# Moving twice as many of the sort's scatters behind the layers' gathers in a four-layer graph network kernel

## The reference

```python
# layer 0: mean of neighbours
mean = segment_sum(x[src], dst) / max(count, 1)
out  = l2_normalise(mean @ W_l + b_l + x @ W_r)
# layer 1: a weight matrix for each edge type
hw   = einsum('ni,rio->rno', x, weight)
out  = relu(segment_sum(hw[type, src] * edge_weight, dst) + bias)
# layer 2: five rounds of a gated cell on a state of 256
m    = h @ W[l];  agg = segment_sum(m[src], dst)
h    = GRU(agg, h)                        # then a two-layer MLP on [h, x]
# layer 3: an MLP on every edge, summed by source
h    = silu([x[src], x[dst], edge_attr] @ eW1 + eb1)
m    = silu(h @ eW2 + eb2)
agg  = segment_sum(m, src)                # then a node MLP on [x, agg]
```

## Time and profile before

| what | value |
|---|---|
| median of three runs | 9513.58 us (9509.02 to 9513.96) |
| the profiled execution's own time | 9513.96 us |
| its span from first to last instruction | 9511.7 us |
| mean granted TensorE clock | 0.819 |
| busy: PE, DVE, ACT, POOL | 64%, 60%, 27%, 72% |
| sort, until the first gather of layer 0 | 0 to 1165.0 us |
| first gathers of layer 1 and of layer 2 | 2210.6 us, 3208.8 us |
| first gather of the edge stage | 8435.2 us |

### The profile page before, as it was taken

One profiled execution on the slowest core, in us unless ns is written; L12 is line 12 of the kernel. 1 busy time (PEld: TensorE's weight loads), 2 busy tenths in 40 slices (PEclk: granted clock), 3 DMA queues, 4 the chain that ended last, 5 costly groups with the idle time before them and its releaser, 6 DMA issues. The chain is left out here.

```text
span 9511.7 us, 154496 instructions
## 1 busy us (share of the span) xinstructions
PE 6059.4 (64%) x34456; PEld 5100.5 (54%) x34457; DVE 5681.1 (60%) x13795; ACT 2535.7 (27%) x6529; POOL 6821.3 (72%) x7393
## 2 busy tenths in 40 slices
PE   0000055554444577777777777777776787779998
PEld 0000043333333466656666566656665666668887
DVE  9999644543444455545555555545554555556666
ACT  4212111112333111111111111111111333346665
POOL 1677377777777777777777777777777766677776
PEclk8555566665555699989999899989998999989999
DMA  2000022222222333333333333333333333322223
GB/s 67 6 7 7 29 78 80 78 78 77 60 60 59 84 111 111 111 98 111 111 111 104 105 111 111 111 98 111 112 111 97 109 100 100 96 54 63 64 64 54
DMA packets 377439, 786.63 MB, mean 83 GB/s; under 512 B 120397, under 2 KB 201394, under 8 KB 376731
## 3 DMA queue, kind: packets, MB, share of 16 engines
q0 software_dynamic: 289440, 677.19, 25.8%
q10 hardware_dynamic: 58500, 64.01, 2.2%
q1 hardware_dynamic: 29173, 42.12, 1.5%
HBM read 698.56 MB, written 84.29 MB: 82 GB/s over the span
## 5 line engine op out<-in xcount | busy, mean ns | idle before, releaser
L937 POOL DMA_INDIRECT rows<-state_table,rec x3910 | 3729.6, 954 | 1278.3 <-issue 1169.7
L1000 PE MATMUL l_prod<-rows,onehot 128*125 x11648 | 2979.0, 410 | 1739.2 <-SPq L949 698.5
L1025 DVE TENSOR_TENSOR agg<-agg,l_prod 125x256 f32 (+2 forms) x5824 | 2235.4, 384 | 2853.6 <-PE l_prod L1000 1889.4
L1000 PEld LDWEIGHTS l_prod<-rows,onehot 128*125 128x125 f32 x11648 | 2232.9, 226 | 2283.4 <-issue 2053.1
L1965 POOL DMA_INDIRECT l_gathered<-xcol_table,l_slots x832 | 785.6, 944 | 264.3 <-issue 250.5
L937 POOL DMA_INDIRECT rows<-rel_table,rec x782 | 738.7, 945 | 247.8 <-issue 237.7
L937 POOL DMA_INDIRECT rows<-in_x_dram,rec x782 | 738.8, 945 | 242.0 <-issue 234.0
L416 POOL DMA_INDIRECT slots_table<-rec_stage,row_stage x560 | 548.5, 980 | 172.4 <-issue 152.9
L1545 PE MATMUL l_rh<-state,w_hh_t 128*128 x4000 | 620.1, 292 | 1.8 <-ACT l_ng L1683 1.8
L1545 PEld LDWEIGHTS l_rh<-state,w_hh_t 128*128 128x128 f32 x4000 | 578.7, 210 | 16.2 <-ACT l_ng L1683 3.4
L1007 DVE TENSOR_TENSOR onehot<-l_rest,rec 128x500 f32<-128x500 f32 x835 | 560.7, 672 | 0.0
(11 more groups left out here) (359 smaller groups left out, 9741.0 us busy)
## 6 DMA issues: line engine op xcount, KB each, us to landing
rows<-state_table,rec POOLq DMA_INDIRECT x3910
rel_table<-l_relrow ACTq DMA_DIRECT2D x50, 500.0 KB
state_table<-l_row ACTq DMA_DIRECT2D x200, 125.0 KB
l_gathered<-xcol_table,l_slots POOLq DMA_INDIRECT x832
rows<-in_x_dram,rec POOLq DMA_INDIRECT x782
rows<-rel_table,rec POOLq DMA_INDIRECT x782
slots_table<-rec_stage,row_stage POOLq DMA_INDIRECT x560, 2.1
slots_table<-fill SPq DMA_DIRECT2D x8, 936.0 KB
```

What stands on the lines that cost most here:

```text
L937: pool.indirect_dma_start(out=K["rows"][:, r, 0:width], out_offset=None, in_=table, in_offset=bass.IndirectOffsetOnAxis(ap=K["rec"][:, c, ...
L1000: last = pe.matmul(p[0:LANES, 0:width], K["onehot"][:, h % ONEHOTS, k, :], rows[:, bass.ds(at[k], width)], start=True, stop=True)
L1025: dve.tensor_tensor(into, into, of, ALU.add).then_inc(S.added, 1)
```

## The change

`LATE` goes from 224 to 448 columns, so that 336 instead of 560 columns are scattered in the sort. Their shares: layer 0 from 44 to 66, layer 1 from 10 to 66, each of the first four rounds of layer 2 from 28 to 66, the last round from 58 to 52. `late_all`, the table `late` and `late_rec` take the new sizes.

```diff
-LATE = 224
-LATE_LAYER0, LATE_LAYER1, LATE_ROUND, LATE_LAST = 44, 10, 28, 58
-assert LATE_LAYER0 + LATE_LAYER1 + 4 * LATE_ROUND + LATE_LAST == LATE
+LATE = 448
+LATE_LAYER, LATE_ROUND, LATE_LAST = 66, 66, 52
+assert 2 * LATE_LAYER + 4 * LATE_ROUND + LATE_LAST == LATE
...
-            late.load(sp, LATE_LAYER0)
+            late.load(sp, LATE_LAYER)
...
-            late.scatter(pool, LATE_LAYER0, 1)
+            late.scatter(pool, LATE_LAYER, 1)
...
-            late.load(sp, LATE_LAYER1)
+            late.load(sp, LATE_LAYER)
...
-            late.scatter(pool, LATE_LAYER1, 2)
+            late.scatter(pool, LATE_LAYER, 2)
...
-                ("late_rec", [128, max(LATE_LAYER0, LATE_LAYER1, LATE_ROUND, LATE_LAST), REC_LATE]))
+                ("late_rec", [128, max(LATE_LAYER, LATE_ROUND), REC_LATE]))
```

## The result

| | median | runs | range |
|---|---|---|---|
| before | 9513.55 us | 4 | 9509.02 to 9513.96 |
| after | 9787.47 us | 4 | 9785.98 to 9798.5 |

The ratio is 1.0293, with a 95% interval from 1.0277 to 1.0308: 273.9 us or 2.9% slower. The forecast was 276.3 us.

The account below looks back on a forecast made before the run. GpSimd's stream of gathers was taken to bound layers 0 and 1 and four rounds, VectorE the sort. Terms 0 + 19.4 + 63.5 + 193.4 + 0 = 276.3 us gave 9790 us, range about 9768 to 9812.

Parts of the forecast that it names:

- What bounds it: Layers 0 and 1 and four of five rounds last as long as GpSimd's gather stream; additions there cost full length.
- Sort, 0: Sort: VectorE sets its end, so 224 fewer GpSimd scatters gain 0; gain bounded by 251 us.
- rival 3: Sort: VectorE was held up by GpSimd, so the sort would shrink by 251 us, to 9539; 2 in 100.
- rival 4: Sort: its end follows GpSimd's, so the barrier comes 324 us earlier, 9466 us, faster; 1 in 100.
- Late pieces on ScalarE, 0: Sort: ScalarE's twice as long late copies and the doubled record write fit in idle time and cover; cost 0.
- Layer 0 to 1 and layer 1 to 2, +19.4 and +63.5: Layer boundaries: added scatters first use up 8.4 and 7.5 us of shadow, then delay the next gather by these amounts.
- shadow left behind the scatters: Layer 0 to 1: time from the last scatter's end to the barrier, 8.4 us, counted as cover for added scatters.
- Rounds, +193.4: Between rounds: no shadow left, so 38 more scatters cost 48.3 us in full, four times.
- Last round to edge stage, 0: Last boundary: six fewer scatters end 7.6 us earlier, but the stores set the barrier, so 0.
- SP and its queue, 0: Rounds: record loads growing from 28 to 66 do not delay GpSimd; 0, bounds 0 and 20 us.
- Rival 1, TensorE's clock: Rounds: longer pauses lower TensorE's clock until it becomes the bound, 130 us more, 9920 us; 6 in 100.
- Rival 2, hidden rounds: Rounds: the drains hide the added scatters, so only layers 0 and 1 pay, 9597 us; 3 in 100.

Follow-up runs that it names:

- e3: Kernel before with 80 more late scatters: layer 0 to 66, layer 1 to 66, last round to 60, rounds kept at 28; 9633.52 us, ratio 1.0110.
- e4: Kernel before with 80 more late scatters, all behind the four rounds (28 to 48 each), layers unchanged; 9636.5 us, ratio 1.0112.
- e1: Kernel before with only a mask (& 255) on the two counts loaded for waits; 9531.95 us, ratio 1.0004 to before.
- e7: Changed kernel's sort side alone: 336 sort scatters, 448 columns loaded, but only 44, 10, 28 four times and 52 scattered late; 9509.71 us, ratio 0.9999 to before.
- e2: Changed kernel with a mask (& 255) added on the two counts loaded for waits; 9818.88 us, ratio 1.0305 to before.
- e5: Kernel before with 192 late scatters instead of 224 (layer 0 42, layer 1 5, rounds 23 each, last 53); 9481.15 us, ratio 0.9970.
- e6: Kernel before with 144 late scatters instead of 224 (layer 0 40, layer 1 2, rounds 14 each, last 46); 9479.51 us, ratio 0.9968.
- e8: Kernel before with GpSimd waiting for its late scatters to land at the ends of layers 0 and 1; 9525.16 us, one run.

## Why the prediction was right, and which step was not

- **What bounds it.** Right for the four rounds and layer 1, and nearly for layer 0, where the trace of before has 15 waits for ring space, 8.0 us in all. The last round, which the prediction did not count among them, waits 70 times for it, 99.7 us. What is put into GpSimd's stream behind the gathers costs its full length: e3 and e4 show 80 scatters at 104.4 and 107.4 us, that is 1.31 and 1.34 each by the medians and 1.27 to 1.30 by the gaps (e4's four rounds +101.8, e3's three boundaries +103.9 over e1).
- **Sort, 0.** Right. e7 isolates it at a ratio of 0.9999. The predicated copy takes 578 ns without scatters beside it, as it did with them. So rival 3 falls, and rival 4 with it: the barrier did not follow GpSimd. The rule of the Trainium skill (SBUF — State Buffer, "Who interferes with whom"), by which two-input VectorE instructions contend with GpSimd's reads, does not appear on VectorE's side in these traces: over a stretch in which GpSimd had been 251 us busy, VectorE's end moved by 1.9 us in the changed kernel (1163.08 to 1161.17) and 1.0 us in e7. Over all traces it lies at 1161.2 to 1162.5 us with 336 scatters in the sort (three) and at 1163.1 to 1163.4 with 560 (three), so a gain of 1 to 2 us is possible, against a bound of 251. Whether GpSimd's issuing of a scatter is a read in the sense of that rule, no run shows.
- **Late pieces on ScalarE, 0.** Right. SP's wait for the longer write is 12.1 us (reckoned 13) and stays inside the cover. The piece grew by 0.78 us (bound +0.97) and the next copy follows without an idle gap, where 0.82 us had been:

```profile
1039.93 1.75 ACT L455 COPY late_all<-attr 128x1792 f32<-128x1792 f32 x1
1041.73 0.60 ACT L488 COPY rec<-rec 112x448 f32<-112x448 f32 x1
```

- **Layer 0 to 1 and layer 1 to 2, +19.4 and +63.5.** The step that failed. I took "shadow left behind the scatters: 8.4 us" and 7.5 us from the distance between scatter and barrier, and gave it to the stores. It belonged to GpSimd's drain and moves with the last scatter. The full counts, 22 x 1.264 = 27.8 and 56 x 1.269 = 71.1, are what was measured: +27.4 and +71.2. e3 confirms it with the rounds left alone (+27.4 and +71.2 over before's trace).
- **Rounds, +193.4.** Right to 0.4 us: +193.0 by the gaps. There is no barrier between rounds, hence no drain, and the reasoning there needed none.
- **Last round to edge stage, 0.** The same failed step with the other sign: "the barrier came 7.2 us after them, with the stores". SP, behind the stores, was 6.6 us earlier, so of the 7.6 us of six scatters some 6.6 could come back. 7.3 did, since the stores themselves came 0.6 us sooner behind the last gather in that execution; e7 gave 6.6. This also went below the bound that I gave ("could give back nothing").
- **SP and its queue, 0.** Right for GpSimd: no wait for the ring appears in the four rounds, though each round's load is 2.4 times as large. e7 shows the load by itself: it loads the 66 records for each round and scatters 28, and its four rounds gather no slower than before's (mean 951 ns of issuing and 0.30 us between, 952 ns before). First the load of e7 in the rounds (KB, us to landing), then its gathers there (count, busy us, mean ns, idle us):

```profile
late_rec<-late_table SPq DMA_DIRECT2D x4, 627.0 KB, 4.1
```

```profile
L937 POOL DMA_INDIRECT rows<-state_table,rec x3128 | 2975.2, 951 | 961.5 <-issue 952.7 <-POOLq L127 8.8
```

- **The sum.** 8.0 and 7.7 us too little at two boundaries and 7.3 us too much at the third cancel in half: 8 us are left between the forecast's 276.3 and the gaps' 284.3. With the step mended the sum is 27.8 + 71.1 + 193.4 - 6.6 = 285.7. That 276.3 met the result's 273.9 to 2.4 us is partly luck. The medians cannot tell the two sums apart: their intervals, 264 to 293 us in the result and 274 to 307 in e2, hold both. The gaps can.
- **Rival 1, TensorE's clock.** It falls. Windows after a pause, before and after (busy us of PE, PEld, DVE, ACT, POOL, then the clock, DMA share, GB/s). The kernel before, first 100 us of its second round and the next 100:

```profile
4227.00:4327.00 100.00, 65.37 (x243) 48.59 (x241) 43.64 (x98) 6.92 (x20) 75.74 (x80) 0.79 0.38 108
4327.00:4427.00 100.00, 81.02 (x459) 69.15 (x457) 61.88 (x143) 19.25 (x59) 75.66 (x80) 0.91 0.39 111
```

  The same of the changed kernel, behind a pause 48 us longer:

```profile
4377.00:4477.00 100.00, 63.31 (x257) 48.49 (x258) 45.83 (x103) 5.63 (x18) 75.61 (x81) 0.79 0.38 111
4477.00:4577.00 100.00, 75.05 (x430) 63.53 (x429) 59.89 (x139) 18.89 (x59) 75.91 (x80) 0.96 0.39 111
```

  The granted clock over the first 100 us is the same 0.79, and GpSimd is as busy as before, 75.6 us of 100.
- **Rival 2, hidden rounds.** It falls with the rounds' 0.30 us between the last scatter and the next gather, and with e4. e5 and e6 show how far off the stores were: with fewer scatters the next gather comes 4 to 8 us sooner, and no more.

Open: the gathers of the four rounds together took 13.1 us more in the profiled execution of the changed kernel (spacing 1.2608 to 1.2614 us, before 1.2556 to 1.2581). e3, whose rounds are those of before, shows 1.258 to 1.259, e6 the same, e5 1.256 to 1.257. e1 and e7 show 1.255 to 1.257, e2 and e4 1.258 to 1.261. So this spacing differs by 0.2 to 0.4% between executions also where a round was not touched. The larger load of late records is not the cause: e7, which has it, gathers at the shorter spacing, and e6, with the smallest load, at the longer one. The cause stays open.

## What to carry to other kernels

Before you call the time between an engine's last instruction and a barrier "shadow", read every engine's arrival at that barrier: only an engine that arrives later than this one gives cover. Work that is moved out of a stage in which its engine has 130 us of slack into one where that engine sets the pace can only cost, and here each piece cost its full issue time; here the better move was the opposite one, up to the point where the stores become the bound (e5, 0.3% faster than before). And when a total comes out as forecast, compare it stage by stage: here a step that was wrong by 8, 8 and -7 us stood behind a total that was off by 2 us.

## What the runs showed of the hardware that was not expected

- GpSimd's DRAIN behind late scatters ends 5.5 us (e6) to 8.4 us (e4) after the end of its last scatter, at the ends of layers 0, 1 and 2 in all runs without an added wait. It is not the landing of the data: with all of it landed beforehand the drain still takes 5.8 and 7.2 us (e8), while SP's takes 7 ns. It repeats to 0.02 us for the same count at layer 1 and at the last boundary, and grows by some 0.08 us for each late scatter added there.
- The pause between rounds has a floor from the last state store: the dependent gather starts 3.4 us after the store is issued (all six gaps of e5 and e6 in which it waited), of which 0.50 us is the issuing.
- The spacing of identical gathers varies by 0.2 to 0.4% from one execution to another (a mean of 951 ns of issuing in e7, 954 in e6, 956 in after), and the same kernel took 9529 us on one chip and 9510 on another.
